# First layer of a two-expert feed-forward kernel by one level of Strassen's algorithm, on one Trainium2 core

## What is computed

```python
def _gated_ffn(x, wi0, wi1, wo):            # wi0, wi1: 512 x 2048, wo: 2048 x 512
    g = jax.nn.gelu(x @ wi0, approximate=True)
    l = x @ wi1
    return g * l @ wo
gate_in = jnp.concatenate([expert_out[:, 0], share_out[:, 0]], axis=-1)
weights = jax.nn.softmax(jax.nn.relu(gate_in @ g0) @ g1, axis=-1)
return x + expert_out * w0 + share_out * w1
```

## Time and profile before

| | before |
|---|---|
| runs | 2107.87 us median of 3 (2107.33 to 2108.17) |
| profiled execution, span | 2106.2 us |
| matmuls | 9225, of 512 columns |
| TensorE busy | 2094.9 us |
| VectorE, ScalarE, GpSimd busy | 945.5, 772.5, 18.7 us |
| read from HBM | 220.21 MB |

### The profile page before, as it was taken

One profiled execution on the slowest core, in us unless ns is written; L12 is line 12 of the kernel. 1 busy time (PEld: TensorE's weight loads), 2 busy tenths in 40 slices (PEclk: granted clock), 3 DMA queues, 4 the chain that ended last, 5 costly groups with the idle time before them and its releaser, 6 DMA issues.

```text
span 2106.2 us, 25050 instructions
## 1 busy us (share of the span) xinstructions
PE 2094.9 (99%) x9225; PEld 1731.9 (82%) x9225; DVE 945.5 (45%) x1310; ACT 772.5 (37%) x1126; POOL 18.7 (1%) x30
## 2 busy tenths in 40 slices
PE   9999999999999999999999999999999999999998
PEld 7888888888888888888888888888888888888886
DVE  4434344453444434444445353444435444444444
ACT  4333333333333333333334333333333333343333
POOL 0000000000000000000000000000000000000000
PEclk9999999999999999999999999999999999999999
DMA  5332233323232232322333323232232422223220
GB/s 190 117 131 96 97 118 112 122 90 108 107 129 106 98 112 99 138 92 104 110 105 130 104 91 119 95 132 102 91 124 90 145 90 103 91 97 137 92 103 35
DMA packets 45775, 229.07 MB, mean 109 GB/s; under 512 B 5154, under 2 KB 6178, under 8 KB 43682
## 3 DMA queue, kind: packets, MB, share of 16 engines
q1 hardware_dynamic: 45730, 228.61, 31.3%
HBM read 220.21 MB, written 8.39 MB: 109 GB/s over the span
## 4 chain that ended last, share of the span: by engine, by line
PE 99%; DVE 0%; POOLq 0%; DMA 0%; POOL 0%; ACT 0%; issue 0%; SPq 0%
PE ps_gate L246 33%; PE ps_lin L246 33%; PE ps_out L277 33%; POOLq L57 0%; DMA x_raw<-x_cols 0%; DVE gate_prod L529 0%; POOL s_out L643 0%; POOL gate_row L635 0%; DVE mix L625 0%; ACT s_out L457 0%; DVE x0l L466 0%; ACT x0h L355 0%; ACT e_out L452 0%; SPq L172 0%; POOL logits L638 0%
## 5 line engine op out<-in xcount | busy, mean ns | idle before, releaser
L489 DVE TENSOR_TENSOR hid<-act,ps_lin 128x512 f32<-128x512 f32 x256 | 176.1, 688 | 896.7 <-PE ps_lin L246 896.0
L382 ACT ACTIVATE act<-ps_gate 128x512 f32<-128x512 f32 x256 | 153.2, 599 | 483.2 <-PE ps_gate L246 482.5
L388 ACT CAST hid0h<-hid 128x512 fp32r<-128x512 f32 x126 | 78.2, 621 | 360.2 <-DVE hid L489 360.2
L388 ACT CAST hid1h<-hid 128x512 fp32r<-128x512 f32 x126 | 78.3, 621 | 351.7 <-DVE hid L489 351.7
L277 PE MATMUL ps_out<-wo0h,hid0l 128*128 128x512 f32 x504 | 196.1, 389 | 0.0
L277 PE MATMUL ps_out<-wo0l,hid0h 128*128 128x512 f32 x504 | 196.1, 389 | 0.0
L277 PE MATMUL ps_out<-wo0h,hid0h 128*128 128x512 f32 x504 | 196.1, 389 | 0.0
L277 PE MATMUL ps_out<-wo1h,hid1l 128*128 128x512 f32 x504 | 196.1, 389 | 0.0
L277 PE MATMUL ps_out<-wo1l,hid1h 128*128 128x512 f32 x504 | 196.1, 389 | 0.0
L277 PE MATMUL ps_out<-wo1h,hid1h 128*128 128x512 f32 x504 | 196.1, 389 | 0.0
L473 DVE TENSOR_TENSOR wi1l<-raw,wi1h 128x1024 fp32r<-128x1024 f32 x128 | 156.8, 1225 | 33.9 <-ACT wi1h L363 33.9
(11 more groups left out here) (137 smaller groups left out, 4137.4 us busy)
## 6 DMA issues: line engine op xcount, KB each, us to landing
raw<-experts SPq DMA_DIRECT2D x128, 768.0 KB, 4.3
raw<-shared SPq DMA_DIRECT2D x126, 768.0 KB, 4.3
x_raw<-x_cols SPq DMA_DIRECT2D x32, 256.0 KB, 5.7
x_res<-x_rows SPq DMA_DIRECT2D x8, 1024.0 KB, 4.8
out<-mix SPq DMA_DIRECT2D x7, 1024.0 KB, 6.8
g_sb<-g_rows SPq DMA_DIRECT2D x1, 2048.0 KB, 8.5
out<-mix SPq DMA_DIRECT2D x4, 256.0 KB, 2.5
raw<-shared SPq DMA_DIRECT2D x4, 128.0 KB, 4.3
```

The costliest lines, as they stand in the source:

```text
L382: nc.scalar.activation(act[s][:, :], ps_gate[s][:, :], ACT.Gelu_apprx_tanh).then_inc(gelu_done, 1)
L388: nc.scalar.copy(hs[slot][HI][:, :], hid[s][:, :]).then_inc(hid_hi_done, 1)
L489: nc.vector.tensor_tensor(hid[s][:, :], act[s][:, :], ps_lin[s][:, :], ALU.mult).then_inc(product_done, 1)
```

## The change

Two chunks are taken together as a step, so that the first layer of a step is a 2 by 2 block product: two chunks by two halves of the features, times two halves of the features by two halves of the tokens. It is computed with seven block products instead of eight. Each is 12 matmuls of 256 columns (gate and linear, 2 blocks of features, 3 passes), so a step has 84 matmuls of 256 columns and, as before, 24 of 512 for the second layer. The order on TensorE is P1, P5, a quarter of the second layer of the step before, P6, P2, quarter, P7, P3, quarter, P4, quarter.

- GpSimd makes four sums of weight blocks for each step and four sums of blocks of `x` for each batch (`weight_sums`, `moving_sums`), each 128x512. They stand in its queue together with the broadcasts and the logit sum.
- ScalarE and VectorE split seven weight operands of 128x512 for each step (`a_hi`, `a_lo`) where before they split two of 128x1024, and seven of `x` for each batch.
- The products are summed partly in PSUM. ScalarE copies P1's bank to `ps_v`, P5's to SBUF, `ps_v` to `ps_p5` and `ps_v` to `ps_c21` for that; VectorE makes two sums of 128x512. Gelu and the products go by quarters of 128x256.
- Weights come by two transfers for each step, `load_wo` (512 KB) into one buffer and `load_w` (1 MB) into one of two.
- The gate's VectorE work is spread over steps 1 to 4 of a shared pass, the mix is done in eight operations of 512 columns, and the second layer is put off only for one step at the end.

The core of the diff, in the order of the engines:

```diff
@@ sync @@
-                        sp.wait_ge(wo_ready, t0 + g * RAW_SLOTS + (r + 1 - RAW_SLOTS))
-                        sp.dma_start(raw[r][:, :], weights(g * RAW_SLOTS + r)).then_inc(raw_loaded[r], 16)
+                for c in range(STEPS):
+                    ahead = c + 1
+                    if not (last and ahead >= STEPS):
+                        sp.wait_ge(wo_ready, (n0 + ahead) * 2)
+                        load_wo(source(net if ahead < STEPS else 1 - net, label, ahead % STEPS))
+                    ahead = c + 2
+                    if not (last and ahead >= STEPS):
+                        sp.wait_ge(a_ready, (n0 + ahead - 1) * PRODUCTS)
+                        load_w(source(net if ahead < STEPS else 1 - net, label, ahead % STEPS), c % 2)
@@ tensor @@
+            def product(i, s, ps, fresh):
+                for a in (GATE, LIN):
+                    for k in range(2):
+                        for h, (ap, xp) in enumerate(PASSES):
+                            mm = nc.tensor.matmul(ps[:, a * HALF:(a + 1) * HALF], a_op[s][ap][:, i, a, k, :],
+                                                  x_op[xp][:, i, k, :],
...
+                operands(P1)
+                    pe.wait_ge(product_done, n * 4 - 3)
+                product(P1, s, ps_c11, True)
+                operands(P5)
+                    pe.wait_ge(c12_done, n)
+                product(P5, s, ps_p5, True)
+                second(0)
+                operands(P6)
+                pe.wait_ge(p1_copied, n + 1)
+                product(P6, s, ps_v, False)
+                operands(P2)
+                product(P2, s, ps_c11, False)
+                second(1)
+                operands(P7)
+                pe.wait_ge(v_copied, n + 1)
+                product(P7, s, ps_v, False)
+                operands(P3)
+                product(P3, s, ps_p5, False)
+                second(2)
+                operands(P4)
+                pe.wait_ge(u_copied, n + 1)
+                product(P4, s, ps_c21, False)
+                second(3)
@@ scalar, one step @@
+                ahead(P1)
+                nc.scalar.copy(ps_v[:, :], ps_c11[:, :]).then_inc(p1_copied, 1)
+                ahead(P5)
+                nc.scalar.copy(p5[:, :, :], halves(ps_p5)).then_inc(p5_saved, 1)
+                ahead(P6)
+                ahead(P2)
+                nc.scalar.copy(ps_p5[:, :], ps_v[:, :]).then_inc(v_copied, 1)
+                wo_hi(n, s, 0, not (first or second))
+                gelu(act[:, GATE, 0, 0:HALF], ps_c11[:, 0:HALF], 1.0)
+                ahead(P7)
+                ahead(P3)
+                wo_hi(n, s, 1, not (first or second))
+                nc.scalar.copy(ps_c21[:, :], ps_v[:, :]).then_inc(u_copied, 1)
+                ahead(P4)
@@ vector, one pass @@
+                for c in range(STEPS):
+                    if c == 1 and not first:
+                        if net == EXPERT:
+                            copy_out(b * 2 + 1, s_out)
+                        else:
+                            copy_out(b * 2, e_out)
+                    step(n0 + c, c % 2, last and c == STEPS - 1,
+                         b + 1 if net == EXPERT and not last and c == STEPS - 1 else None)
+                    if net == EXPERT and c == 3:
+                        gate_half(b, 0, SHARED)
+                    if net == SHARED and not first:
+                        if c == 1:
+                            gate_half(b - 1, 1, EXPERT)
+                            gate_logits(b - 1)
+                        if c == 2:
+                            shift_logits(b - 1)
+                        if c == 3:
+                            gate_weights(b - 1)
+                            combine_shared(b - 1)
+                        if c == 4:
+                            combine_expert(b - 1)
@@ gpsimd @@
-            for b in range(BATCH):
-                for n, net_out in enumerate((s_out, e_out)):
-                    pool.wait_ge(out_copied_act, b * 2 + (n + 1))
-                    nc.gpsimd.partition_broadcast(gate_row[:, n, :], net_out[0:1, 0, :]).then_inc(row_spread, 1)
+            def weight_sums(m, s, lap, first=False):
+                    pool.wait_ge(w_loaded[s], lap * 16)
+                    pool.wait_ge(a_ready, m * PRODUCTS + (P5 + 1 - PRODUCTS))
+                add(sums[:, S1, :, :, :], a_block(s, 1, 0), a_block(s, 1, 1), ALU.add, sums_done)
+                add(sums[:, S2, :, :, :], sums[:, S1, :, :, :], a_block(s, 0, 0), ALU.add, sums_done)
+                add(a_block(s, 1, 0), a_block(s, 1, 0), a_block(s, 0, 0), ALU.add, sums_done)
+                add(sums[:, S4, :, :, :], sums[:, S2, :, :, :], a_block(s, 0, 1), ALU.add, sums_done)
+            def one_pass(b, net):
+                for c in range(STEPS):
+                    n = n0 + c + 2
+                    if n < N_STEPS:
+                        weight_sums(n, c % 2, n // 2 + (c % 2))
+                    if net == EXPERT:
+                        if c == 1:
+                            spread(b, 0, s_out)
+                        if c == 3 and not last:
+                            moving_sums(b + 1)
+                    elif not first:
+                        if c == 1:
+                            spread(b - 1, 1, e_out)
+                        if c == 2:
+                            sum_logits(b - 1)
+            weight_sums(0, 0, 0, first=True)
+            moving_sums(0, first=True)
+            weight_sums(1, 1, 1)
```

More of the change, by code:

```diff
@@ L261, in project @@
-            def project(t, s, xslot, second=False):
-                pe.wait_ge(wi_ready, t)
-                for which, bank_, free, done in ((0, ps_gate[s], gelu_done, gate_projected),
-                                                 (1, ps_lin[s], product_done, lin_projected)):
-                    if not second:
-                        pe.wait_ge(free, t - 1)
-                    for k in range(KC):
-                        mm = project_k(bank_, which, k, s, xslot)
-                    mm.then_inc(done, 1)
@@ new lines, in one_pass, with last_step, operands @@
+            def one_pass(b, net, n0, first, last):
+                for c in range(STEPS - 1 if last else STEPS):
+                    ends = b * 2 + (1 if net == EXPERT else 0)
+                    step(n0 + c, c % 2, c, b, net == SHARED and c == 0, first and c == 0, first and c == 1, ends)
+            def last_step(n):
+                s = 1
+                def operands(i):
+                    pe.wait_ge(a_ready, n * PRODUCTS + (i + 1))
+                operands(P1)
+                pe.wait_ge(product_done, n * 4 - 3)
+                product(P1, s, ps_c11, True)
+                operands(P5)
+                pe.wait_ge(c12_done, n)
+                product(P5, s, ps_p5, True)
+                pe.wait_ge(hid_ready, n * 2)
+                pe.wait_ge(wo_ready, n * 2)
+                down(0, 0, False, False)
+                operands(P6)
+                pe.wait_ge(p1_copied, n + 1)
+                product(P6, s, ps_v, False)
+                operands(P2)
+                product(P2, s, ps_c11, False)
+                operands(P7)
+                pe.wait_ge(v_copied, n + 1)
+                product(P7, s, ps_v, False)
+                operands(P3)
+                product(P3, s, ps_p5, False)
+                operands(P4)
+                pe.wait_ge(u_copied, n + 1)
+                product(P4, s, ps_c21, False)
+                down(1, 0, False, False)
+                down(2, 0, False, False)
+                pe.wait_ge(hid_ready, n * 2 + 2)
+                pe.wait_ge(wo_ready, n * 2 + 2)
+                down(0, 1, False, True).then_inc(last_down_done, 1)
+                down(3, 0, False, False)
+                for m in range(1, MC):
+                    down(m, 1, False, True).then_inc(last_down_done, 1)
@@ L449, in _ @@
+            for i in range(PRODUCTS):
+                a_hi(0, 0, i, 0, False, first=True)
+                x_hi(0, i, None)
+            schedule(sc, one_pass)
             nc.scalar.activation(exp_warm[:, :], logits[:, 0:1], ACT.Exp)
@@ L610, in _ @@
+            nc.vector.memset(idle[:, :], 0.0).then_inc(idle_ready, 1)
+            for i in range(PRODUCTS):
+                a_lo(0, 0, i)
+                x_lo(0, i)
+            schedule(dve, one_pass)
+            gate_half(BATCH - 1, 1, EXPERT)
+            gate_logits(BATCH - 1)
             shift_logits(BATCH - 1)
```

682 lines of the change are left out of this document (373 added, 309 removed).

## The result

| | before | after |
|---|---|---|
| runs | 2107.6 us beside it | 2406.45 us median of 4 (2402.18 to 2410.99) |
| ratio | | 1.1416, 95% interval 1.14 to 1.1432 |
| profiled execution, span | 2106.2 us | 2409.2 us |
| matmuls | 9225 | 13834 |

The change makes the kernel slower by 14%. The forecast was 2350 in a range of 2190 to 2460. The sign, the range and most mechanisms hold; how the 299 us are made up does not, and one of the rivals describes GpSimd and VectorE better than the forecast did.

A forecast was written before the change was run, and what follows sets the result against it. TensorE, 99% busy, was taken to bound the kernel. Steps 1986.5, start 22.2 and end 13.1 make 2021.8; +136.5 +24 +35 +8 +21 = 2246; +90 = 2336, forecast as 2350 with the median's offset and dearer program changes; range 2190 to 2460.

The forecast's parts named there:

- TensorE's step: TensorE, each step: 84 matmuls at 0.120 plus 24 at 0.2266 make 15.52 us; 128 steps are 1986.5.
- Start and end: Kernel's first step and its tail after the last output: 22.2 us more than the work, and 13.1 us.
- Mix, exponential, row work and splits of x: VectorE and ScalarE work beside the steps of each batch: 35 + 8 + 21 us.
- Change of program: GpSimd switching between sums and broadcasts or reductions, 6.8 us each way: 136.5 us in shared passes, 24 in expert passes.
- second rival: GpSimd's change toward the broadcast costs nothing, only the way back 6.8: 46 instead of 136.5, total 2222; chance 0.13.
- GpSimd beside VectorE: Sums and splits reading SBUF side by side in ordinary steps: 0 to 177 us, the middle, 90, taken.
- The rival that shuts both out: GpSimd and VectorE exclude each other in SBUF, splits of 693 ns turning to over 1000: 2423 or 2435; chance 0.20.
- The loop through the loads: Weight landing, GpSimd's sums, splits, wo_ready, next load: 13.9 us a turn, 1.6 to spare against the 15.52 step.
- both nearly free: GpSimd's program changes cost almost nothing once programs have been loaded, 6.79 being only a first use: about 2085; chance 0.12.
- paced by weight loads: TensorE's 256-column matmuls take their weight load's 0.188 each: 21.2 us a step, over 2750 in all; chance 0.05.

The follow-up runs named there:

- Writes only with early loads: Changed kernel with first-layer weights loaded ahead of the wo_ready wait and GpSimd's block sums replaced by fills that read nothing; 2048.96 us, ratio 0.9718.
- The kernel of one program: Changed kernel, late load, with GpSimd's broadcast and logit sum replaced by tensor_tensor additions, so its program never changes; 2301.85 us, ratio 1.0917.
- the writes-only kernel: Changed kernel, late load, with each GpSimd sum replaced by three fills of zeros that read nothing; 2148.19 us, ratio 1.0188.
- small transfers: Changed kernel with gate row and logits spread through DRAM on SyncE's queue, GpSimd keeping one program; 2300.6 us with late loads, 2175.75 with early loads.

## Why the prediction was right, and where it was wrong

- **TensorE's step.** Right. A matmul of 256 columns costs 0.120 as forecast, and weight loads hide. A detail is off: in the changed kernel those of 512 columns take 0.232 and not 0.2266, so the step is 15.65 and not 15.52. Writes only with early loads fits it: 16 steps would be 250.4, its batches follow each other in 251.4. The gap formula of the Trainium skill (TensorE: Matmul & The Clock Gate, Back-to-back issue gap), which the page gives for a matmul by itself, makes 0.109; the trace, where each has its own weight load, does not agree.
- **Start and end.** 35.3 forecast. In that kernel 2047.7 less 128 x 15.65 and 7 x 1.0 leave 37.5.
- **Mix, exponential, row work and splits of x: 64 forecast, 9 for each batch.** Too much where nothing else is late: 1.0 for each batch in that kernel, where the splits are not stretched. With GpSimd reading, spreading the mix, together with moving the load of `x_res` and the sums of the next `x`, still brought 20.
- **Change of program.** The mechanism is as forecast, both ways and in every excursion: 47 pairs of MODIFY_POOL_CONFIG against some 46 forecast, 22 waits of 131.0 us in all ahead of broadcasts and reductions, and the two long steps with TensorE standing (9.0 and 5.6 us, forecast about 10). VectorE's waits of 12.6 forecast for the row are 13.3 in the mean (106.4 over 8). The term was 136.5 + 24 = 160.5, and taking the change away gave 104.6, or 50.1 with early loads. Most of that difference is not an error of the price: the 136.5 holds VectorE's whole stand, and by the forecast's own second rival 46 of it stay when the way toward costs nothing, because the row stands behind the four sums. The kernel of one program shows that part (VectorE still waits 8.0 us for the row in the mean). The other 12.9 for each shared pass are some 12 in the step lengths (29.1 + 23.6 against 23.0 + 17.3, means of seven), and the expert pass is 4 instead of 3.
- **GpSimd beside VectorE: 90 forecast, between 0 and 177.** This term failed: its size, and the choice of the middle. With the late load it is 154. I took the middle of my bounds because no row stood nearer; what happens is the upper end's mechanism, in which the two engines take turns. The upper end was added wrongly besides: 5.3 + 4 x 0.6 is 7.7 and not 7.0, which makes the bound some 255 us instead of 177; the four sums took 6.4 (105.39 to 111.78). The rival that shuts both out predicted splits of over 1000 ns in place of 693, and 989 to 1181 are the means in the trace, with both queues moving one operation each 1.7 us (an estimate from these rows: 0.6 of a split and 1.1 of a sum). The Trainium skill (SBUF — State Buffer, Who interferes with whom) states this exclusion, for a VectorE instruction with two inputs in SBUF and a GpSimd instruction that reads; the trace agrees, and the writes-only kernel shows that it takes the reads. That it takes two inputs in SBUF is seen in the kernel with the early load: `act<-ps_v,p` (L585), with one input in PSUM, took 676 to 693 ns in all its 128 instances, though most of them ran beside a sum, while splits there took up to 1.80 us.
- **The loop through the loads.** The forecast found the loop, with 13.9 us against 15.52 and 1.6 to spare, and charged it only through the stretched sums. It is 16.1 in an ordinary step and binds. The transfer was near (0.37 and 5.95 against 6.5). Wrong is the way from the sums back to the load: I had all four sums and then three splits, 5.3 + 2.1. The path in the trace leaves GpSimd after the second sum (2.9), and then goes through VectorE's own order, 0.6 on ScalarE and 3.28 + 0.60 + 1.28 + 0.61 for splits, two of them stretched, because the second layer's split, for which SyncE waits, stands behind them. More important is what I did not ask: how much of the loop must be there at all. The load stood behind a wait that it has nothing to do with, for 14.4 us, and the exchange of the two loads gives 248 us back.
- **The sum.** The forecast's terms, sorted as the runs separate them: without company and without the change, but with the row behind the sums, 2087 + 46 = 2133; that kernel took 2148, 15 more. The change was 114 with 12 as a margin, and is 104.6: 22 too high. The company was 90 and is 153.7: 64 too low. Together that makes the difference between 2350 and 2406, to within 1. So the forecast is off mainly by one term. That the 15 fit so well is in part luck, since the 64 for mix and `x` were too much and the late load, which alone costs 99 in that kernel, was not in the sum.
- **The rivals.** One way free (2222) and both nearly free are refuted by the 5.57 and 7.94, paced by weight loads by the 0.12. The 2085 of the third was for a kernel without either cost; that kernel took 2148 with the late load, and 2049 only with the early one. Exclusion (2423, or 2435) is the rival whose mechanism the trace shows, and it lies nearer to 2406 than the forecast's 2350.

Open remains why ordinary steps are 16.1 us in one part of each batch and 17.5 to 17.8 in another; in the longer ones the load lands in 6.9 to 7.5 us instead of 5.9. Whether the landing is the cause was not tested; one program leaves both as they are, and with writes only most of both are 15.6. Nor was it tested why small transfers cost nothing with late loads and some 67 us with early ones; VectorE's waits above fit it.

## What to carry to other kernels

Fewer multiplications pay only if the operands come free: here seven products instead of eight were worth 2.6%, and what feeds them turned that into a loss of 14%, since the sums put a third engine and one more hop in the loop that reloads the weights. Look in each queue for an instruction that stands behind a wait it does not need, and put loads ahead of such waits before tuning anything else; but when an instruction is moved forward, work out when its queue gets there, or it blocks what stood behind. Where costs share a loop, measure them in a table with and without each other, not one by one.

## What the runs showed of the hardware

- VectorE operations with two operands in SBUF and GpSimd sums that read SBUF took turns: 688 ns became up to 1.78 us, 1.25 us became 1.74. GpSimd writes of the same 512 columns left VectorE at 688 ns, and were themselves 526 ns. VectorE operations of 128x512 with one input in PSUM stayed at 676 to 693 ns beside the sums.
- A change of GpSimd's program took 5.6 to 6.5 us toward the broadcast or the reduction in the changed kernel, before all 22 that came behind a sum and not only at first use. Back it took 7.1 to 7.9 in the nine places where no wait covered it, and 7.2 to 9.9 in the kernel with the broadcasts ahead of the sums. Between writes and broadcasts the trace shows none. At the start nothing of it is seen: the pair stands at 1.0 us, and the first sum began at 6.76, as soon as its load had landed.
- In the kernel that also has 256-column matmuls those of 512 columns started 0.232 us apart, also behind one of 512; in the kernel before it was 0.2266. Why was not tested.
